# A vision block on one core: leaf rows of two trees added on VectorE before one turn, one TensorE signal for two halves, and a new order

## The reference

```python
h = patches @ tok_W.T + tok_b                      # 64 x 196 x 256
z = layernorm(h)
xn = z / max(norm(z) * 256**-0.5, 1e-5) * g
uv = silu(xn @ uv_w.T); u, v, base = uv[:512], uv[512:1024], uv[1024:]
q, k = rope(base * gamma[0] + beta[0]), rope(base * gamma[1] + beta[1])
kern = square(relu((q @ k.T + w_rel[j - i]) / sqrt(128)))
h = h + z * res_scale + (u * (kern @ v)) @ o_w.T
y = layernorm(h)
logits = y @ W_in.T + b_in                         # 8 trees of depth 7, 255 nodes each
acts = silu(logits)                                # a logit over 0 goes right
h = h + (acts of the 8 nodes that a token visits in each tree, else 0) @ W_out.T
```

## Time and profile before

| | |
|---|---|
| median of 3 runs | 2202.95 us (2196.44 to 2209.55) |
| profiled execution: its time, its span | 2201.36 us, 2199.5 us |
| mean granted TensorE clock | 0.981 of full |
| TensorE busy | 2066.1 us, 94%, 13256 matmuls |
| VectorE busy | 1621.5 us, 74% |
| ScalarE busy | 1395.2 us, 63% |
| GpSimd busy | 774.1 us, 35% |
| DMA | 163.13 MB, mean 74 GB/s |

### The profile page before, as it was taken

How to read it: one execution, slowest core, us unless ns; L and a number is a source line. 1 busy time by engine, 2 the same in 40 slices (tenths; PEclk the granted TensorE clock), 3 DMA queues, 4 the chain that set the end, 5 groups by cost and what they waited for, 6 DMA issues and landing times.

```text
span 2199.5 us, 42461 instructions
## 1 busy us (share of the span) xinstructions
PE 2066.1 (94%) x13256; PEld 1941.8 (88%) x13256; DVE 1621.5 (74%) x4210; ACT 1395.2 (63%) x3085; POOL 774.1 (35%) x905
## 2 busy tenths in 40 slices
PE   6899999999999999999999999999999999999997
PEld 5789889899988898888998898988889988889887
DVE  5678777777777787777777777777777877777775
ACT  5556666666666566566666665666665666656654
POOL 2752333232333333332323333323323233333233
PEclk8999999999999999999999999999999999999999
DMA  5331322222322223222223222222223232222222
GB/s 146 85 94 52 89 73 66 73 76 63 83 71 65 81 55 84 75 64 73 77 62 84 70 73 73 64 75 77 65 70 84 55 85 69 73 73 66 63 67 74
DMA packets 81999, 163.13 MB, mean 74 GB/s; under 512 B 17102, under 2 KB 48048, under 8 KB 81968
## 3 DMA queue, kind: packets, MB, share of 16 engines
q0 software_dynamic: 40960, 103.02, 17.4%
q1 hardware_dynamic: 41008, 59.71, 9.3%
HBM read 148.76 MB, written 13.90 MB: 74 GB/s over the span
## 4 chain that ended last, share of the span: by engine, by line
PE 84%; another core or an unknown queue 5%; ACT 4%; POOL 3%; issue 2%; DVE 1%; DMA 1%; ACTq 0%; POOLq 0%; SPq 0%; DVEq 0%
PE front L1142 10%; PE front L1144 9%; PE front L1143 9%; PE hid_ps L1142 9%; PE hid_ps L1143 9%; PE hid_ps L1144 9%; PE out_acc L1142 6%; PE out_acc L1143 6%; PE out_acc L1144 6%; PE out_acc L1378 4%; PE front L1177 2%; PE front L1184 2%; PE hid_ps L1366 2%; PE hid_ps L1337 2%
## 5 line engine op out<-in xcount | busy, mean ns | idle before, releaser
L474 POOL DMA_INDIRECT leaf_rows<-leaf_table,leaf_at x512 | 532.4, 1040 | 163.9 <-issue 163.4
L453 POOL TENSOR_TENSOR inv_root<-to_root,minus_half 98x8 f32<-98x8 f32 x64 | 111.0, 1734 | 728.3 <-DVE to_root L885 404.6
L528 ACT ACTIVATE hid_hi<-hid 128x392 fp32r<-128x392 f32 (+1 forms) x256 | 177.8, 695 | 237.1 <-PE out_acc L1144 155.4
L1142 PE MATMUL out_acc<-hid_hi,outw_lo 128*128 128x392 f32 x768 | 293.4, 382 | 2.6 <-DVE hid_lo L835 2.3
L1142 PE MATMUL hid_ps<-ffn_x,in_lo 128*128 128x392 f32 x768 | 282.3, 368 | 6.2 <-POOL in_lo L445 5.8
L1143 PE MATMUL hid_ps<-ffn_x,in_hi 128*128 128x392 f32 x768 | 266.3, 347 | 0.0
L1144 PE MATMUL hid_ps<-ffn_x,in_hi 128*128 128x392 f32 x768 | 264.7, 345 | 0.0
L1144 PE MATMUL out_acc<-hid_hi,outw_hi 128*128 128x392 f32 x768 | 264.6, 345 | 0.0
L1143 PE MATMUL out_acc<-hid_lo,outw_hi 128*128 128x392 f32 x768 | 264.4, 344 | 0.0
L473 POOL TENSOR_TENSOR held<-minus_half 98x1 f32<-98x1 f32 x128 | 47.2, 369 | 489.9 <-issue 428.7
L718 ACT ACTIVATE leaf_rows<-leaf_rows,leaf_act 98x256 f32<-98x256 f32 x512 | 218.2, 508 | 0.1
(11 more groups left out here) (140 smaller groups left out, 5808.2 us busy)
## 6 DMA issues: line engine op xcount, KB each, us to landing
x_raw<-x SPq DMA_DIRECT2D x192, 196.0 KB, 2.4
out<-out_stage SPq DMA_DIRECT2D x32, 392.0 KB
leaf_rows<-leaf_table,leaf_at POOLq DMA_INDIRECT x512
leaf_table<-leaf_rows SPq DMA_DIRECT2D x4, 256.5 KB, 4.7
out_stage<-in_w SPq DMA_DIRECT2D x4, 256.0 KB
tok_major<-tok_w SPq DMA_DIRECT2D x3, 256.0 KB, 4.3
late_raw<-out_w SPq DMA_DIRECT2D x6, 128.0 KB
u<-uv_w SPq DMA_DIRECT2D x1, 576.0 KB, 4.2
```

Source lines behind the costliest of these rows:

```text
L453: pool.tensor_tensor(inv_root[:, 0:size], to_root[:, 0:size], minus_half[:, 0:size], ALU.pow).then_inc(roots_ok, 1)
L474: pool.indirect_dma_start(row_slot(s, g), None, table, bass.IndirectOffsetOnAxis(ap=leaf_at[:, s, g:g + 1], axis=0), element_offset=s * P ...
L528: act.activation(out, src, ACT.Copy).then_inc(done, 1)
L1142: pe.matmul(out, w[1], x_parts[0], start=start, stop=False)
```

## The change

Three things are changed together.

First, the rows of the gathered trees are added in couples (0 and 1, 2 and 3). `scale_rows` stays for trees 0 and 2. For trees 1 and 3 the new `merge_rows` on VectorE multiplies the row by its activation and adds the scaled row of the tree before, into the slot of the second. `add_rows` is called for trees 1 and 3 alone. The fetch of an even tree now waits for the merge, that of an odd tree for `add_rows`.

```diff
+COUPLES = GATHERED // 2
...
                     if GROUPS * (s + 1) > ROW_SLOTS or not first(i):
-                        pool.wait_ge(rows_added, GATHERED * i + s + 1 - ROW_SLOTS // GROUPS)
+                        couple = COUPLES * i + (s // 2 + 1 - ROW_SLOTS // GROUPS // 2)
+                        if s % 2 == 0:
+                            pool.wait_ge(rows_merged, GROUPS * couple)
+                        else:
+                            pool.wait_ge(rows_added, couple)
                     if s > 0 or not first(i):
...
+            def merge_rows(i, s):
+
+                if i is None:
+                    return
+                dve.wait_ge(leaf_active, GATHERED * i + s + 1)
+                dve.wait_ge(rows_scaled, GROUPS * (COUPLES * i + s // 2 + 1))
+                for g in range(GROUPS):
+                    one, two = (row_slot(n, g)[:, ROW_IN:ROW] for n in (s - 1, s))
+                    dve.scalar_tensor_tensor(two, two, leaf_act[:, s, g:g + 1], one,
+                                             ALU.mult, ALU.add).then_inc(rows_merged, 1)
...
                     return
-                pe.wait_ge(rows_scaled, GROUPS * (GATHERED * i + s + 1))
+                pe.wait_ge(rows_merged, GROUPS * (COUPLES * i + s // 2 + 1))
                 for m in range(DC):
                     for g in range(GROUPS):
                         at = slice(ROW_IN + m * P, ROW_IN + (m + 1) * P)
```

Second, TensorE raises one signal where it raised one for each half: `embed` after steps 2 and 5 of 6, `turn_h`, the turns back and `tree_out` after the second half, `tree_logits` after a tree's last half. The waits on these count accordingly; 54 signals a unit are left. Some of the places:

```diff
+X_SIGNALS = (2, 5)
...
                 if m == 0:
-                    act.wait_ge(x_used, n * XC + XC)
+                    act.wait_ge(x_used, 2 * n + 2)
...
                     return
-                act.wait_ge(ffn_x_turned, 2 * n + m + 1)
+                act.wait_ge(ffn_x_turned, n + 1)
...
                                    k == 0, k == XC - 1)
-                last.then_inc(x_used, 1)
+                if k in X_SIGNALS:
+                    last.then_inc(x_used, 1)
...
-                last.then_inc(h_turned, 1)
+                if m == DC - 1:
+                    last.then_inc(h_turned, 1)
...
-                last.then_inc(done, 1)
+                if m == DC - 1:
+                    last.then_inc(done, 1)
...
                     last = product(hid_ps[:, t % 2, b, 0:T], w, (ffn_x[:, 0, m], ffn_x[:, 1, m]),
                                    m == 0, m == DC - 1)
-                last.then_inc(logits_ready, 1)
+                if b == halves(t) - 1:
+                    last.then_inc(logits_ready, 1)
...
                                    t == 0 and b == 0, t == TREES - 1 and b == halves(t) - 1)
-                last.then_inc(tree_added, 1)
+                if m == DC - 1:
+                    last.then_inc(tree_added, 1)
```

Third, the lists of the engines are new. TensorE's:

```diff
             def body(p, i, n, nx):
+                tree_logits(p, 4, 1)
+                find_leaf(p, 3)
+                tree_out(p, 1, 1)
+                make_v(i, 1)
+                make_v(i, 2)
+                tree_out(p, 2, 0)
+                tree_visits(p, 4)
+                make_v(i, 3)
+                tree_logits(p, 5, 0)
                 make_u(i, 0)
                 make_u(i, 1)
-                tree_visits(p, 4)
                 tree_logits(p, 5, 1)
                 scores(i, 0)
+                tree_logits(p, 6, 0)
                 scores(i, 1)
-                tree_out(p, 3, 0)
+                add_rows(p, 1)
                 make_u(i, 2)
+                tree_out(p, 2, 1)
+                tree_logits(p, 6, 1)
                 make_u(i, 3)
-                tree_logits(p, 6, 0)
-                add_rows(p, 1)
                 mix(i, 0)
-                tree_visits(p, 5)
-                tree_logits(p, 6, 1)
                 mix(i, 1)
                 mix(i, 2)
+                tree_visits(p, 5)
+                tree_out(p, 3, 0)
+                tree_out(p, 3, 1)
+                mix(i, 3)
+                tree_out(p, 4, 0)
                 tree_visits(p, 6)
-                mix(i, 3)
-                tree_out(p, 3, 1)
-                tree_out(p, 4, 0)
                 project_o(i, 0, range(0, 3))
                 project_o(i, 0, range(3, EC))
                 project_o(i, 1, range(0, EC))
-                embed(n, 0)
+                tree_out(p, 4, 1)
                 turn_h(i, 1, 0)
                 turn_h(i, 1, 1)
-                tree_out(p, 4, 1)
+                embed(n, 0)
                 embed(n, 1)
+                embed(n, 2)
                 tree_logits(p, 7, 0)
                 tree_logits(p, 7, 1)
-                embed(n, 2)
                 embed(n, 3)
                 embed(n, 4)
                 embed(n, 5)
-                add_rows(p, 2)
                 turn_ffn_x(i, 0)
                 turn_ffn_x(i, 1)
+                tree_visits(p, 7)
                 tree_out(p, 5, 0)
-                tree_visits(p, 7)
                 tree_out(p, 5, 1)
                 turn_h(n, 0, 0)
                 turn_h(n, 0, 1)
+                if first(n):
+                    turn_rows()
                 tree_logits(i, 0, 0)
+                tree_logits(i, 1, 0)
                 tree_out(p, 6, 0)
+                add_rows(p, 3)
+                tree_visits(i, 0)
                 tree_out(p, 6, 1)
-                tree_visits(i, 0)
-                tree_logits(i, 1, 0)
-                tree_logits(i, 2, 0)
-                add_rows(p, 3)
-                find_leaf(i, 0)
                 tree_visits(i, 1)
                 tree_out(p, 7, 0)
+                find_leaf(i, 0)
+                tree_logits(i, 2, 0)
                 tree_logits(i, 3, 0)
                 find_leaf(i, 1)
+                tree_out(p, 7, 1)
                 tree_visits(i, 2)
-                if first(n):
-                    turn_rows()
-                tree_out(p, 7, 1)
-                tree_logits(i, 4, 0)
                 turn_xn(n, 0)
                 turn_xn(n, 1)
+                tree_logits(i, 4, 0)
+                tree_visits(i, 3)
                 tree_out(i, 0, 0)
-                tree_out(i, 0, 1)
                 find_leaf(i, 2)
                 turn_normed(n, 0)
+                turn_normed(n, 1)
+                tree_out(i, 0, 1)
                 tree_out(i, 1, 0)
-                turn_normed(n, 1)
-                tree_visits(i, 3)
                 make_base(n)
-                tree_logits(i, 4, 1)
                 make_v(n, 0)
-                make_v(n, 1)
-                tree_out(i, 1, 1)
-                tree_logits(i, 5, 0)
-                find_leaf(i, 3)
-                make_v(n, 2)
-                tree_out(i, 2, 0)
-                make_v(n, 3)
-                add_rows(i, 0)
-                tree_out(i, 2, 1)
```

ScalarE's, from `silu_base` to the third `silu_u`:

```diff
                 silu_base(n)
+                silu_v(n, 0)
                 scale_base(n, 1)
+                leaf_number(i, 3)
                 scale_base(n, 0)
-                leaf_silu(i, 0)
-                silu_v(n, 0)
                 silu_v(n, 1)
-                scale_rows(i, 0)
+                silu_tree(i, 4, 1)
                 v_high(n, 0)
                 v_high(n, 1)
+                silu_tree(i, 4, 0)
+                leaf_silu(i, 0)
                 qk_high(n, 0)
+                silu_v(n, 2)
                 qk_high(n, 1)
-                silu_v(n, 2)
                 silu_v(n, 3)
-                v_high(n, 2)
-                leaf_number(i, 3)
-                hid_high(i, 3)
-                silu_tree(i, 4, 1)
-                silu_tree(i, 4, 0)
+                scale_rows(i, 0)
                 leaf_silu(i, 1)
                 silu_u(n, 0)
+                v_high(n, 2)
+                v_high(n, 3)
                 silu_u(n, 1)
-                v_high(n, 3)
-                scale_rows(i, 1)
-                hid_high(i, 4)
-                if first(n):
-                    build_rows()
+                x_high(nx, 0)
+                x_high(nx, 1)
+                hid_high(i, 3)
+                x_high(nx, 2)
                 kern_high(n, 0)
                 kern_high(n, 1)
+                hid_high(i, 4)
                 silu_u(n, 2)
```

VectorE's, from `residual` to the mixes, and its end:

```diff
                 residual(n, 0)
                 residual(n, 1)
+                hid_low(i, 2)
+                mask(i, 3)
+                leaf_dots(i, 0)
                 decisions(i, 4)
-                leaf_dots(i, 0)
-                mask(i, 3)
                 rotate_qk(n, 1)
-                hid_low(i, 2)
                 rotate_qk(n, 0)
                 v_low(n, 0)
                 v_low(n, 1)
+                mask(i, 4)
+                if first(n):
+                    build_toward()
+                leaf_dots(i, 1)
                 qk_low(n, 0)
                 qk_low(n, 1)
-                leaf_dots(i, 1)
-                if first(n):
-                    build_toward()
-                hid_low(i, 3)
+                merge_rows(i, 1)
                 v_low(n, 2)
-                mask(i, 4)
                 add_rel_bias(n, 0)
                 square_relu(n, 0)
                 add_rel_bias(n, 1)
+                square_relu(n, 1)
+                hid_low(i, 3)
+                kern_low(n, 0)
                 v_low(n, 3)
```

(34 more changed lines are left out.)

70 lines of the change are left out of this document (28 added, 42 removed).

## The result

The change made the kernel slower: 2260.66 us (median of 4 runs) against 2203.7 us for the kernel before, ratio 1.0267 with a 95% interval of [1.0219, 1.0315]. The forecast was 2076 us, range 2025 to 2180.

What follows compares the result with a forecast made beforehand. TensorE, busy 94% of the span, was taken as the bound. From 2201.4 us: minus 43.5 (turns), 91.5 (both waits) and 17 (clock), plus 27 (waits that stay), gives 2076 us; range 2025 to 2180.

Steps and rivals of the forecast that it cites:

- Turns, 43.5 us: Leaf-row transposes on TensorE: half of them go, 64 calls of 0.68 us saved, 43.5 us.
- ScalarE and VectorE: Row scaling: ScalarE loses 109 us, VectorE gains 108 us at 0.42 us a merge, hidden behind TensorE's other work.
- The two waits, 91.5 us: TensorE's waits before make_base and before the second make_v, for late signals: 48.2 + 43.3 us, counted as removed.
- the 27 that were to stay: What remains of the gaps before make_base and the second make_v: 0.44 and 0.43 us a unit, 27 us.
- d: Lateness of TensorE's signal, taken as 0.9 us for the last turn and 2.0 us for the base.
- a queue of 0.65 us a signal: From last turn of xn to last of normed: signals queue at 0.65 us each; four, not seven, should not build up.
- Rival B: Around the two waits: fewer signals don't help, lateness stays 2.93 and 3.07 us; 33 us more waits, 2191 us; chance 0.08.
- down by 17: Half-clock windows after TensorE's longer gap: 0.56 us a unit, 17 us over 31 units, counted as saved.
- Fetches of trees 2 and 3 at nothing: Leaf-row fetches now issued eight in a row: costed at nothing, with a bound of 1 us a unit, 32 us.
- rival C: Mix stage: eight fetches in a row make signals late there, 4.6 us a unit, 142 us, total 2218 us; chance 0.10.
- Signals cost TensorE no time: TensorE's matmul increments: 23 of 77 signals fewer, no direct saving counted; the skill's 26 ns would give 19 us.
- Readers of first halves at nothing: Consumers of a first half now start when the second is done: costed at nothing, without cover 16 us.

Runs made afterwards that it cites:

- b_merge4: Kernel before with merged rows, tree 2's leaf products moved later, tree 3's gathers held until the last gate, tree 1's until the base's activation; 2101.7 us.
- a_nogather: Kernel after with the gathers of the leaf rows done for the first unit alone; 2044.2 us.
- b_nogather: Kernel before with the gathers of the leaf rows done for the first unit alone; 2058.4 us.
- a_plain: Kernel after with each gather replaced by a plain transfer of as many bytes at the same place; 2038.7 us.
- a_pairs77: a_split with 77 signals a unit, and tree 0's third and fourth gathers held until VectorE has read the turned rows; 2060.4 us.
- b_sig59: Kernel before with 59 signals a unit, halves paired except at the embedding and the turns before make_base; 2299.4 us.
- a_sig77: Kernel after with 77 signals a unit for 54, each half signalling by itself again; 2318.4 us.
- a_nostore: Kernel after storing only one of 128 partitions of each unit, gathers as they are; 2246.3 us.
- a_split1: Kernel after with GpSimd holding tree 1's four gathers until the base's activation, parting the first run of eight; 2210.6 us.
- a_split: a_split1 with tree 3's gathers also held until the last gate and tree 3's leaf products moved behind the second norm's moments; 2104.0 us.
- a_pairs54: a_pairs77 with 54 signals a unit, one for each pair of halves; 2081.0 us.
- b_sig54: Kernel before with the 54 signals a unit alone, one for each pair of halves; its order, rows and gathers stay; 2443.9 us.
- b_split1: Kernel before with one wait added: GpSimd holds tree 1's four gathers until the base's activation; 2090.7 us.

## Why the prediction was wrong

*Turns, 43.5 us.* The count was right (512 transposes). What they alone are worth no run shows: without gathers all three changes together gain 1.05 us a unit for the turns' 1.36, and in the old order the merged rows gain nothing (b_merge4). In all it is 14 us, since the new order also starts later (first store at 166.9 for 156.9 in the versions without gathers). That later start, 13.3 us in the full kernel, has no term in my sum.

*ScalarE and VectorE.* ScalarE lost 101.5 us for 109 and VectorE's merges follow each other after 0.40 us (477 ns long, overlapped) for 0.42. Right, and hidden.

*The two waits, 91.5 us, and the 27 that were to stay.* Here the prediction failed. Its gaps, d − 0.46 and d − 1.57, were good: with the d that was measured, 1.93 and 3.84, they give 1.47 and 2.27 for 1.52 and 2.16. Wrong was d itself, 0.9 and 2.0, and with it the sentence that a queue of 0.65 us a signal should not build up with four signals for seven. The lateness hangs on the gathers: there is none without them (a_nogather, b_nogather), none with plain transfers (a_plain), and with all 77 signals hardly any where the gathers lie otherwise (a_pairs77, 3 of 1960). Under gathers the signals do queue, but at no fixed rate: some 0.73 us apart at first in the kernel before, 1.4 to 2.9 in b_sig59, so fewer signals ahead of a turn did not bring its own out earlier there, though in the new order fewer signals are worth 58 us (a_sig77 against the kernel after). The evidence against me stood in the prediction, under B: the base's signal came 2.75 us after the last turn and was still 3.07 late.

*Rival B* (lateness belongs to the stretch, 2191 us) named the mechanism closest: 113.8 us of waits against its 91.5 + 33 = 124.5. Of the 65 us from 2191 to 2256 the late start is 13.3 and the wait at the visits 10.1. The half-clock stretches went up by 22 us instead of down by 17, but a_nostore shows that they don't simply add. The rest is not placed.

*Fetches of trees 2 and 3 at nothing, and rival C.* C had the place and the cause, eight gathers over the mixes. In the kernel after they make a signal 2.26 us late but stop TensorE little, the wait at the visits of 10.1 us among it. In a_split1, with the first run parted, TensorE waits 45.3 us for the gates, and parting the second run as well is worth 107 us (a_split1 to a_split), against C's 142. I priced B and C each by itself; that the first run's waits cover the second in the kernel after is my reading and not shown.

*Signals cost TensorE no time.* The Trainium skill, TensorE: Matmul & The Clock Gate, section "The cost: per-tile semaphore tail", gives some 26 ns an increment; by it a_pairs54 should have been an estimate of 17 us below a_pairs77. It is 21 above, so no such gain is seen; whether one lies hidden under the longer waits, this pair can't tell. *Readers of first halves at nothing*: the 54 signals cost 21 to 26 us where runs are short, above my bound of 16, and far more in the old order (b_sig54), but late signals are part of that, and the readers' share is not taken apart.

## What to carry to other kernels

When a consumer on another engine starts late though its producer is done, look at what GpSimd does at that moment before counting signals: here one wait that holds back four of eight gathers was worth 5.7% (b_split1). A change that ties the release of buffers together, as a merge of two trees' rows does, also ties together the transfers that refill them; ask how many will be issued in a row and which signals lie under them. Take apart a mechanism that two rows suggest before it becomes the largest term of a sum: a version without the gathers would have shown 4.59 us a unit at once.

## What the runs showed of the hardware

Indirect transfers issued by GpSimd held TensorE's signals in these kernels. In the loop 312 of 1888 signals were over 0.15 us late in the kernel before, 308 of 1294 after, none with plain transfers of the same bytes on the same queue and none without gathers. Where a run held signals, the hold began with its third or fourth gather (one each 1.28 us) and ended about 1.5 us after the last, and the held signals came out one by one. Other runs, of up to eight, held nothing; what decides that besides the number in a row, no run shows. The latest signal in the loop came 4.2 us behind its matmul in the kernel after, and 6.15 in b_sig59. The Trainium skill, Perfetto Trace Analysis, section "DMA Instruction — SWDGE (GPSIMD)", says that the end shown for such a transfer is that of descriptor generation and not of the data; the lateness that goes on after the last gather's end agrees with that, but why a signal of another engine is held, and why plain transfers of the same bytes hold none, no run here shows.

The half clock came with long waits, though not in step with them: from 300 to 2000 us the lost clock is 22.2 us before, 44.4 after, 13.7 in a_nostore, where TensorE stood longer than in the kernel after, and nothing in a_split, b_split1 and a_pairs77.
